# The passage from the convolution to the first LSTM unit: loads issued in another order, last gelu cut in two, sums on a semaphore of their own

## What is computed

```python
    x = L0_attn_r
    x = x + _layernorm(_L0_attn_ref(_layernorm(x, axis=-1), ...), axis=-1)
    x = x + _layernorm(_L0_ffn_ref(_layernorm(x, axis=-1), ...), axis=-1)

    # attn: a convolution along the 2048 positions, then
    return jax.nn.gelu(y1, approximate=False)

    # ffn
    def step(c, xt):
        ft = jax.nn.sigmoid(xt @ wf.T + c @ uf.T + bf)
        it = jax.nn.sigmoid(xt @ wi.T + c @ ui.T + bi)
        gt = jnp.tanh(xt @ wc.T + c @ uc.T + bc)
        c = ft * c + it * gt
        return (c, None)
    h = jnp.tanh(jnp.einsum('tbi,oi->tbo', x, wo) + c_final @ uo.T + bo)
```

## Time and profile before

| | us |
|---|---|
| median of 3 runs | 2644.72 (2644.36 to 2645.83) |
| the profiled execution: device time | 2645.57 |
| its span, first to last instruction | 2643.90 |
| PE busy | 2527.1 (96%) |
| DVE / ACT / POOL busy | 1837.5 / 1626.2 / 1128.8 |
| granted TensorE clock, mean | 0.983 |

### The profile page before, as it was taken

How to read it: one execution, slowest core, us unless ns; L and a number is a source line. 1 busy time by engine, 2 the same in 40 slices (tenths; PEclk the granted TensorE clock), 3 DMA queues, 4 the chain that set the end, 5 groups by cost and what they waited for, 6 DMA issues and landing times.

```text
span 2643.9 us, 57576 instructions
## 1 busy us (share of the span) xinstructions
PE 2527.1 (96%) x22659; PEld 2202.8 (83%) x22659; DVE 1837.5 (70%) x3409; ACT 1626.2 (62%) x3013; POOL 1128.8 (43%) x1433
## 2 busy tenths in 40 slices
PE   5499999997899999999999999999999999999998
PEld 4278888886788888888888888888888888888887
DVE  7855556558887677776777887777677774467667
ACT  8756667566655555555556665555555554379777
POOL 7778686725332223222234332322222320068667
PEclk9799999998999999999999999999999999999999
DMA  8769797889674455445665755544456432489998
GB/s 352 291 230 315 265 314 271 269 296 341 181 196 116 129 141 164 124 116 127 146 164 149 195 161 142 168 123 116 126 140 163 127 85 49 157 333 352 367 360 347
DMA packets 507551, 542.52 MB, mean 205 GB/s; under 512 B 273936, under 2 KB 412944, under 8 KB 488720
## 3 DMA queue, kind: packets, MB, share of 16 engines
q1 hardware_dynamic: 507280, 538.85, 65.2%
HBM read 292.88 MB, written 180.88 MB: 179 GB/s over the span
## 4 chain that ended last, share of the span: by engine, by line
PE 84%; POOL 4%; DVE 4%; ACT 3%; DMA 3%; issue 2%; SPq 1%; DVEq 0%; POOLq 0%; ACTq 0%
PE bank L2162 31%; PE bank L2172 29%; PE bank L2218 8%; PE bank L2051 4%; PE bank L2001 3%; PE bank L2037 3%; PE bank L2059 2%; PE bank L2013 2%; PE bank L2193 2%; DVE big L1843 1%; PE bank L2021 1%; POOL big L891 1%; ACT big L1354 1%; POOL big L995 1%; DMA x1d<-big 1%
## 5 line engine op out<-in xcount | busy, mean ns | idle before, releaser
L2162 PE MATMUL bank<-big 128*128 128x256 f16 x8064 | 1081.0, 274 | 19.7 <-ACT big L1400 8.6
L2172 PE MATMUL bank<-big 128*128 128x256 f16 x7056 | 962.7, 273 | 0.0
L2162 PEld LDWEIGHTS bank<-big 128*128 128x128 f16 x8064 | 789.7, 98 | 118.6 <-ACT big L1400 9.9
L2172 PEld LDWEIGHTS bank<-big 128*128 128x128 f16 x7056 | 689.7, 98 | 80.5
L1036 POOL TENSOR_SCALAR big<-big 128x1 f32<-128x1 f32 x253 | 108.2, 427 | 1086.9 <-DVE big L1690 807.7
L1900 DVE TENSOR_TENSOR big<-bank,big 128x512 f32<-128x512 f32 x256 | 174.9, 683 | 198.2 <-PE bank L2172 194.6
L2218 PE MATMUL bank<-big 128*128 128x256 f16 x2688 | 295.5, 273 | 4.4 <-ACT bank L1334 4.0
L1310 ACT ACTIVATE big<-big 128x512 f32<-128x512 f32 x384 | 289.5, 803 | 14.1 <-DVE big L1900 14.1
L2218 PEld LDWEIGHTS bank<-big 128*128 128x128 f16 x2688 | 261.8, 98 | 37.8 <-ACT bank L1334 5.0
L1886 DVE TENSOR_TENSOR big<-bank,big 128x512 f32<-128x512 f32 x256 | 176.2, 688 | 141.6 <-PE bank L2172 119.8
L1242 ACT ACTIVATE big<-big 128x512 f32<-128x512 f32 x256 | 206.0, 808 | 101.4 <-POOL big L1038 98.0
(11 more groups left out here) (234 smaller groups left out, 3719.5 us busy)
## 6 DMA issues: line engine op xcount, KB each, us to landing
xtd<-big SPq DMA_DIRECT2D x60, 1024.0 KB, 6.6
big<-xr SPq DMA_DIRECT2D x16, 2048.0 KB, 9.1
big<-xg SPq DMA_DIRECT2D x64, 512.0 KB, 8.0
big<-kpad SPq DMA_DIRECT2D x32, 1024.0 KB, 12.1
yd<-big SPq DMA_DIRECT2D x16, 2048.0 KB, 16.7
big<-x SPq DMA_DIRECT2D x128, 256.0 KB, 3.3
x1d<-big SPq DMA_DIRECT2D x128, 256.0 KB, 3.2
big<-x1d SPq DMA_DIRECT2D x64, 512.0 KB, 8.8
```

Source lines behind the costliest of these rows:

```text
L2162: ins = e.matmul(o, WX[2 * g + lw][:, q, kt, 128 * a:128 * a + 128], slot[u % 2][:, part, lx, k0 + kt, :], start=(first and kt == 0 and (l ...
L2172: ins = e.matmul(o, WC[2 * g + lw][:, q, kt, 128 * a:128 * a + 128], cc[unit(u)[1] % 2][:, qc, lx, kt, :], start=False, stop=end, skip_gro ...
```

## The change

It has six parts.

1. **Order of loads on SP.** At the head of round `i == NG`: `fbs`, the four x tiles of unit 0, `WX[4]`, `WX[5]`, `WC[0]`, then `load_y(0)` and the store of group 14. Before, `load_y(0)` stood first, the x tiles and `fbs` behind it, and the three weight blocks after the x tiles of unit 1. `load_y(1)` moves ahead of the last two `store_x1` of unit 0; `WC[1]` ahead of the x tiles of unit 1.
2. **Slot signals.** `store_xt(v)` signals `xs{v % 2}` (both halves) in place of `xs0`, `xs1` by half; a turn of unit v waits for the store that last read its slot, and SP no longer waits for `store_xt(0)` before it issues `store_xt(1)`.
3. **Last gelu in two parts**, batch row 0 first. DVE and PE go on after that part, the store of group 15 after both. The statistics of group 15 read `Y[1]` directly, and the copy of group 15 into `yt` moves from DVE to ACT, behind a dummy sigmoid. PE's bias products no longer wait for the gelus.
4. **Sums on own semaphore.** `first_sums(1)` on POOL counts on `fs` and starts without waiting for DVE's `first_sums(0)`; every count on `ss` is 4 less.
5. **Three products between the transposes.** Group 0's products 4, 1 and 2 come after the sixth turn; the seventh and eighth turn and the wait for all low halves follow.
6. The semaphore `kscl` is given up for `gs`, in the work before the convolution.

```diff
-        def first_sums(ss, p):
+        def first_sums(ss, p, name):
...
-            ss().tensor_tensor(s1, b0, b1, ADD).then_inc(s["ss"], 1)
+            ss().tensor_tensor(s1, b0, b1, ADD).then_inc(s[name], 1)
...
             def store_y(g):
-                w.wait_ge(s["gl"], 8 * g + 8)
+                w.wait_ge(s["gl"], 8 * g + 8 + (g == NG - 1))
...
+                if i == NG:
+                    w.wait_ge(s["cv"], G * (NG - 1))
+                    w.wait_ge(s["accs"], 16 * 3)
+                    e.dma_start(fbs, accd.rearrange("g p h -> p g h")).then_inc(s["accs"], 16)
+                    for c in CHUNKS:
+                        load_x1(0, c)
+                    w.wait_ge(s["wx"], 16 * 4)
+                    load_WX(4)
+                    load_WX(5)
+                    load_WC(0)
+                    load_y(0)
+                    store_y(NG - 2)
...
                 if v >= 2:
                     w.wait_ge(s["p7"], 6 * (v - 1))
-                    w.wait_ge(s[f"xs{k // 2}"], 16 * (v - 1))
+                    w.wait_ge(s[f"xs{v % 2}"], 32 * (v // 2))
...
                 if v == 1:
                     store_xt(0)
                     load_WC(5)
-                    w.wait_ge(s["xs0"], 16)
-                    w.wait_ge(s["xs1"], 16)
                 if v < NU - 2:
                     store_xt(v)
...
-            ps.last, ps.count["ss"] = "ss", 4
-            first_sums(ps, 1)
+            first_sums(Chain(w, s, "fs"), 1, "fs")
...
+                    if n < 8 * NG - 1:
+                        e.activation(oy, iy, ACT.Gelu, scale=scale[:, 8:9]).then_inc(s["gl"], 1)
+                    else:
+                        e.activation(oy[:, :, 0:1], iy[:, :, 0:1], ACT.Gelu, scale=scale[:, 8:9]).then_inc(s["gl"], 1)
+                        e.activation(oy[:, :, 1:8], iy[:, :, 1:8], ACT.Gelu, scale=scale[:, 8:9]).then_inc(s["gl"], 1)
...
             e.activation(junk, in_c[:, 0:1], ACT.Sigmoid)
+            w.wait_ge(s["gl"], 8 * NG)
+            w.wait_ge(s["cv"], G * (NG - 1))
+            w.wait_ge(s["yc"], 1)
+            e.activation(yt[:, NG - 1], Y[1][:, 0, 0:4, :], ACT.Copy).then_inc(s["yc"], 1)
...
-            e.tensor_copy(yt[:, NG - 1], Y[1][:, 0, 0:4, :]).then_inc(s["yc"], 1)
...
-                    w.wait_ge(s["yc"], 2)
-                    pr().bn_stats(st0[n][:, 6:12], yt[:, NG - 1, c, :]).then_inc(s["pr"], 1)
+                    pr().bn_stats(st0[n][:, 6:12], Y[1][:, 0, c, :]).then_inc(s["pr"], 1)
...
                     if n == 0:
-
+                        turn(6)
+                        turn(7)
                         w.wait_ge(s["xlo"], 8)
-                    step(n, 2, Bn[:, 0:256], True)
```

More of the change, by code:

```diff
@@ L601, in load_WC, with load_y, load_x1 @@
                 e.dma_start(WC[n].rearrange("p q k f -> p q (k f)"), wg[2 * g + 1][:, l]).then_inc(s["wc"], 16)
+            def load_y(v):
+                b, j = unit(v)
+                src = yd[:, :, b, 4 * j:4 * j + 4, :].rearrange("g t k h -> t g k h")
+                if v == 0:
+                    w.wait_ge(s["y0"], 16 * 7)
+                    w.wait_ge(s["y1"], 16 * 7)
+                    e.dma_start(yt[:, 0:NG - 2], src[:, 0:NG - 2]).then_inc(s["yl"], 16)
+                    return
+                w.wait_ge(s["y0"], 16 * 8)
+                w.wait_ge(s["y1"], 16 * 8)
+                if v == 1:
+                    w.wait_ge(s["yc"], 2)
+                elif v == 2:
+                    w.wait_ge(s["x1"], 4)
+                    w.wait_ge(s["yl"], 32)
+                else:
+                    w.wait_ge(s["ss"], 8 * v - 4)
+                    w.wait_ge(s["xh"], 8 * v - 2)
+                    w.wait_ge(s["xlo"], 8 * v - 2)
+                e.dma_start(rows_y(v), src).then_inc(s["yl"], 16)
+            def load_x1(v, c):
+                b, j = unit(v)
+                if v == 1:
+                    w.wait_ge(s["x2"], 4)
+                    w.wait_ge(s["xl%d" % c], 32)
+                elif v:
+                    w.wait_ge(s["xh"], 8 * (v - 1) + 4 * (c % 2) + 4)
+                    w.wait_ge(s["xlo"], 8 * (v - 1) + 4 * (c % 2) + 4)
+                e.dma_start(xb[c], x[b, 512 * j + 128 * c:512 * j + 128 * c + 128, :]).then_inc(s[f"xl{c}"], 16)
             e.dma_start(sm, small).then_inc(s["sm"], 16)
@@ L670, in sync_program @@
                     weights(j)
[L672 to L682, removed]
-                    w.wait_ge(s["yc"], 2)
[L684 to L697, removed]
-                    w.wait_ge(s["x2"], 4)
-                    w.wait_ge(s["xl%d" % c], 32)
-                elif v:
-                    w.wait_ge(s["xh"], 8 * (v - 1) + 4 * (c % 2) + 4)
-                    w.wait_ge(s["xlo"], 8 * (v - 1) + 4 * (c % 2) + 4)
-                e.dma_start(xb[c], x[b, 512 * j + 128 * c:512 * j + 128 * c + 128, :]).then_inc(s[f"xl{c}"], 16)
             def store_x1(v, r):
@@ L786, in sync_program @@
             w.wait_ge(s["fb"], 12)
-            load_WC(0)
             load_WC(1)
+            for c in CHUNKS:
+                load_x1(1, c)
             w.wait_ge(s["fb"], 20)
@@ L832, in sync_program @@
                 w.wait_ge(s[f"xq{c}"], 32 * (NU - 1))
-            w.wait_ge(s["xs0"], 16 * (NU - 2))
-            w.wait_ge(s["xs1"], 16 * (NU - 2))
+            for r in range(2):
+                w.wait_ge(s[f"xs{r}"], 16 * (NU - 2))
             e.dma_start(Uo, wd).then_inc(s["wu"], 16)
@@ L2134, in pe_program, with turn @@
                     e.matmul(bank[0][:, 4 * g + m:4 * g + m + 1], fbs[:, g, 128 * m:128 * m + 128], one[:, 0:1], start=True, stop=True).then_inc(s["fb"], 1)
-            for i in range(8):
+            w.wait_ge(s["gl"], 8 * NG + 1)
+            def turn(i):
                 v, p, k = item(i)
@@ L2147, in pe_program @@
                         ins.then_inc(s["fb"], 1)
+            for i in range(6):
+                turn(i)
             w.wait_ge(s["yc"], 3)
```

55 lines of the change are left out of this document (23 added, 32 removed).

## The result

The changed kernel takes 2658.12 us in the median against 2644.72 before. The ratio is 1.0044 [1.0031, 1.0056], that is 11.6 (8.2 to 14.8) us more. (One disturbed run of 6263.40 us is counted in that median but not in the ratio; the other four lie at 2654.27, 2655.88, 2658.12 and 2658.29, with a median of 2657.00, 12.3 us over before.) The forecast was 2654, the range 2646.5 to 2658.5. The profiled execution is the quickest of them, 2654.27 with a span of 2652.5, against 2645.57 and 2643.9: +8.7.

What follows compares the result with a forecast made beforehand. The point where PE becomes steady (683.93 us) was taken to set the end; terms 11.3 - 0.3 + 1.4 - 2.3 - 1.0 = +9.1 us gave 2654.7 profiled, say 2654 on the median; 8-in-10 range 2646.5 to 2658.5.

Steps and rivals of the forecast that it cites:

- What bounds the kernel: Step: the point where PE becomes steady, 683.93 us before the change, moves the end by as much as it moves.
- `load_y(0)` behind 4.59 MB: Largest term, head of unit 0's chain: the load lands at 603.4, DVE's statistics start 11.3 us later.
- Copy off DVE, gelu: Term in unit 0's chain: the copy leaving DVE gives -0.3 us, the split gelu 0 under the late load.
- Three products and sums: Term at unit 0's last turns: the last low half ends 0.1 to 2.6 us later, taken as +1.4.
- Unit 1's list: Term: DVE's preparation of unit 1 starts 12.4 us late, gives back 2.3; PE restarts 10.1 us late.
- 1.08 us wait for PE at 631.09: Part of unit 1's give-back: DVE's wait goes because PE has its weights sooner, -1.1 us.
- the lighter queue: Part of unit 1's give-back: 2.75 MB less behind it on SP, up to 2.3 us more could go.
- Slot signals: Term at unit 2's x1 stores: SP issues about 6 us sooner, landing 1 us sooner (0 to 2), so -1.0.
- The sum: All terms together: +9.1 us, 2654.7 for the profiled execution, say 2654 on the median; ends 2648.6 to 2658.1.
- Rival (c): Clock stays low for all of unit 0's beginning, nothing given back: +13.4, 2658; chance 0.08 including beyond.
- (a): Rival at unit 2: freed x1 store removes three waits for ACT, 6.9 us; shift +3.2, 2647.9; chance 0.20.
- (b): Rival at unit 0: load_y(0) overtakes the bulk loads; -2.5, 2642.2, or with (a) 2636.3; chance 0.10.

Runs made afterwards that it cites:

- e8_changed_again: The changed kernel run once more without an edit: 2657.26 us, ratio 1.0049 to the kernel before.
- e1_y_first: The changed kernel with load_y(0) moved back ahead of fbs, the x tiles and the three weight blocks: 2651.45 us, ratio 1.0027 to the kernel before.
- e11_y_before_wc0: The changed kernel with one weight block, WC0 (0.92 MB), moved behind load_y(0): 2654.95 us, ratio 1.0042 to the kernel before.
- e6_best_guess: The kernel before with wd store late, slot signals, split gelu, copy on ACT and sums on fs, without the three products: 2643.44 us, ratio 0.9996.
- e5_wd_late: The kernel before with the 1 MB store of wd moved behind the store of y group 15: 2643.51 us, ratio 0.9995.
- e7_best_three: e6_best_guess plus the three products between the sixth and seventh turn: 2645.22 us, ratio 1.0002 to the kernel before.
- e12_fs_only: The kernel before with only POOL's first sums of the second half on their own semaphore fs: 2644.53 us, ratio 1.0001.
- e2_slots_only: The kernel before with the slot signals alone: 2645.19 us, ratio 1.0003.
- e9_x1_first: e5_wd_late with two x1 stores of unit 2 issued ahead of the xt store of unit 0 and WC5: 2640.31 us, ratio 0.9986 to the kernel before.

## Why the prediction was right

Slower by more than 0.2% was forecast, with 2654; measured were 2658.12 (2657.00) and, run again, 2657.26; the ratio's interval times 2644.72 is 2652.9 to 2659.5. The cause and the largest term were right; two smaller terms were too favourable. Step by step:

**What bounds the kernel.** That the point at which PE becomes steady sets the end held in all traces: from unit 2 to the end 1952.4 to 1952.8 us.

**`load_y(0)` behind 4.59 MB: +11.3.** Measured 9.7 + 2.0 = +11.7 at the statistics, 11.8 in e8_changed_again. Counted from the issue of the `wd` store, the statistics start 20.55 us after it for 8.86, again +11.7. It lands at 602.3 (602 to 605 was named), and the wait is 20.49 us ("some 20"). That bytes ahead in the queue are the cause is shown by taking them away: all of them in e1_y_first (-10.9), 0.92 MB in e11_y_before_wc0 (-2.0).

**Copy off DVE, gelu: -0.3 and 0.** Measured -0.15 at the first `bn_aggr`, 0 else under the late load. With the cover gone the two are worth 0.6 us there (0.6 us after the convolution's end in e6_best_guess, 1.25 in e5_wd_late), within the 0.7 that was given as their most, but only 0.1 us at the first turn, since ACT's own list comes next.

**Three products and sums: +1.4.** From the first turn to the last low half it took 13.1 and 13.6 us in the changed kernel for 11.6 before: +1.4 and +1.9. Half clock for the products, "wholly or in part", was seen both ways (2.29 and 2.77 us). The size held, and as the net of both parts, as it was reckoned: the last two turns wait for nothing any more, but they stand behind the products. Taken apart, the three products cost 2.2 (e7_best_three against e6_best_guess), and `fs` without them gives back 0.4 in e12_fs_only and up to 1.1 in e6_best_guess against e5_wd_late. These single prices are good to about 1 us, for the moment at which the clock comes back differs between the traces. That POOL's sums slow DVE's by 1.0 us was not foreseen; in the changed kernel it hid behind DVE's wait of 2.17 us for ACT at 623.89.

**Unit 1's list.** It started 12.3 us late (13.0 in e8), forecast 12.4. It gave back 1.4 to 1.6 us, forecast 2.3: PE's restart is 10.9 and 11.4 us late, forecast 10.1. This is the term that was mis-sized, in both of its parts. Of the 1.08 us wait for PE at 631.09 0.56 stayed, in both traces of the changed kernel, so it gave 0.5 and not 1.1: PE had the weights but itself waited 1.34 us for ACT at 636.57. The rest, which was put down to the lighter queue, gave 0.9 and 1.1 for 1.2, and part of that was a shorter wait for POOL's sums. The "up to 2.3 us more" that stood for the queue had no row of its own.

**Slot signals: -1.** This gain is not shown. Alone there are 0.6 at unit 2, less than two traces of one kernel differ, and nothing in the median. In the whole change 65.6 to 107.1 is 1.2 us shorter than before, in e8 0.2 us longer; but PE's waits in that stretch are 7.4 us for 7.5, and the 1.2 are the clock's (its shortfall, added up as above, is 5.2 us for 6.3). And the x1 store does not land sooner: POOL starts its sums 19.3 us after PE's restart at unit 1, before 19.4. The reason given, bytes and not SP, was right (e2_slots_only, e9_x1_first), and by it the gain should have been nothing.

**The sum.** Forecast +9.1. At unit 2 the traces have +9.7 and +11.6, the medians +12.3 (2657.00) and +12.5, with an interval from +8.2. So the forecast lies low, by about 0.8 us in the give-back and by up to 1 us in the slot signals; the rest is within what two traces of one kernel differ and is not resolved by these runs. The median of 2658.12 lies only 0.4 us inside the wide range's end of 2658.5 and at the end of the narrow one (2658.1), so that it falls inside is in part luck. Rival (c), that the clock stays low and nothing comes back, did not come about: in e8_changed_again the clock came back some 1 us later, and still 1.6 us were given back.

**Rivals (a) and (b)** fell by e2_slots_only (and the 7.38 us wait after) and by e1_y_first with e11_y_before_wc0. The rule that stood beside (b), from the Trainium skill (DMA: Bandwidth & Descriptors, Queues, rings and completion order), was not seen to act here: from the `wd` store to the last y store, in the traces of before and after, the transfers landed in order of issue. The rule says that a DMA on few rings may complete ahead of an earlier one on more; it does not say that this load would be served beside the bulk, so (b) had less behind it than the prediction gave it.

## What to carry to other kernels

A small load that heads a chain belongs ahead of the bulk in its queue: each megabyte before it costs by the queue's rate (here 0.92 MB cost 2.0 us), and calling a load early does not make it early if the queue's order puts it late. Before moving up work that starts a chain, ask for the next starter and for the last transfer that the chain meets: here 4.7 us at the head gave nothing, since the gelu came next, and what was won behind it was lost at a store which waited in the queue; only with that store ahead of the bulk did the time fall, in one run by shorter waits and in the other by a clock that stayed up. And two engines set to work side by side can cost each other what the overlap was to bring.

## What the runs showed of the hardware that was not expected

DVE's `tensor_tensor` of 128x256 float32 with both inputs in SBUF takes 0.42 us alone and 0.97 and 0.84 while POOL does the same operation (0.72 and 0.79 us), in e12_fs_only. The Trainium skill (SBUF — State Buffer, Who interferes with whom) says that VectorE with two SBUF inputs and a GpSimd operation that reads SBUF exclude each other, and the second blocks until the first is done. The rows agree in kind: 0.42 plus the rest of POOL's operation, 0.68 and 0.55 us, would be 1.10 and 0.97, in both cases 0.13 us above what is seen. DVE's next operations, with one input in PSUM, took 0.65 us each beside POOL.
